# Halves of the convolution result split ahead of its transposes, low halves on GpSimd, weight pieces and x in a new order

## The reference

```python
h = conv1d(x, weight, taps=9, groups=4, pad=4) + (cond @ c_weight.T)[:, :, None] + bias
x = x + attention(h)      # q, k, v, o from 4-bit codes and scales, RoPE, 32 query heads, 8 kv heads
att = softmax(mlp(cond))  # 8 kernels mixed per sample
x = x + ffn(mix(att) @ x) # 512x512 base matmul plus top-2 of 28 LoRA experts
```

## Time and profile before

| | |
|---|---|
| median of 3 runs | 1658.37 us (1656.62 to 1659.03) |
| profiled execution, its own time | 1658.53 us |
| its span, first to last instruction | 1656.7 us |
| PE busy over the span | 1608.9 us, 97% |
| DVE, ACT, POOL busy | 84%, 76%, 68% |
| first block | 0 to 90 us |
| attention steps and the rest | 90 to 1656.7 us |

### The profile page before, as it was taken

How to read it: one execution, slowest core, us unless ns; L and a number is a source line. 1 busy time by engine, 2 the same in 40 slices (tenths; PEclk the granted TensorE clock), 3 DMA queues, 4 the chain that set the end, 5 groups by cost and what they waited for, 6 DMA issues and landing times.

```text
span 1656.7 us, 37682 instructions
## 1 busy us (share of the span) xinstructions
PE 1608.9 (97%) x14847; PEld 892.3 (54%) x14848; DVE 1397.7 (84%) x2174; ACT 1251.2 (76%) x2158; POOL 1130.7 (68%) x942
## 2 busy tenths in 40 slices
PE   8869999999999999999999999999999999899998
PEld 7825555555555555555555555555555555566665
DVE  4758888888888888888888888888888888888887
ACT  2348888888888888888888888888888888642221
POOL 1038777877787778777877787778777787623332
PEclk9989999999999999999999999999999999999999
DMA  8310010001000100000001000100000003012221
GB/s 302 93 45 27 14 33 2 27 14 33 1 27 15 33 1 27 14 33 2 27 14 33 2 27 15 33 1 24 17 1 27 25 2 89 27 64 89 78 79 50
DMA packets 31021, 60.83 MB, mean 37 GB/s; under 512 B 11368, under 2 KB 13992, under 8 KB 29568
## 3 DMA queue, kind: packets, MB, share of 16 engines
q1 hardware_dynamic: 30848, 58.42, 11.0%
HBM read 47.46 MB, written 10.95 MB: 35 GB/s over the span
## 4 chain that ended last, share of the span: by engine, by line
PE 66%; DVE 16%; POOL 6%; issue 5%; ACT 1%; DVEq 0%; POOLq 0%
PE banks L812 17%; PE banks L727 16%; PE banks L752 10%; DVE q_sin L1052 9%; PE banks L868 5%; PE banks L741 5%; DVE accT L1115 4%; PE banks L771 4%; PE banks L797 3%; PE banks L889 2%; DVE pT L1101 2%; PE banks L853 2%; POOL q_f L1312 2%; PE banks L839 1%; POOL k_f L1297 1%
## 5 line engine op out<-in xcount | busy, mean ns | idle before, releaser
L727 PE MATMUL banks<-hT,w_q 128*128 128x512 f16 x2048 | 549.3, 380 | 8.7 <-ACT banks L1432 3.7
L1432 ACT ACTIVATE banks<-banks,ratios 128x512 f32<-128x512 f32 x768 | 503.3, 663 | 65.9 <-PE banks L727 56.8
L812 PE MATMUL banks<-o_hl,w_o 128*128 128x512 f16 x2048 | 545.0, 380 | 3.0 <-ACT banks L1442 1.4
L1442 ACT ACTIVATE banks<-banks,ratios 128x512 f32<-128x512 f32 x768 | 480.8, 659 | 44.4 <-PE banks L812 41.6
L1312 POOL TENSOR_TENSOR q_f<-q_f,q_sin 128x1024 f32<-128x1024 f32 x128 | 301.4, 2355 | 100.8 <-DVE q_sin L1052 100.8
L812 PEld LDWEIGHTS banks<-o_hl,w_o 128*128 128x128 f16 x2048 | 180.7, 98 | 262.6 <-issue 35.3
L1052 DVE TENSOR_TENSOR q_sin<-banks,rope_q 64x1024 f32<-64x1024 f32 x256 | 312.7, 1222 | 8.2 <-POOL q_f L1312 2.5
L727 PEld LDWEIGHTS banks<-hT,w_q 128*128 128x128 f16 x2048 | 188.8, 98 | 240.4 <-ACT banks L1432 39.4
L1043 DVE TENSOR_SCALAR banks<-banks,ratios 128x512 f32<-128x512 f32 x192 | 145.2, 756 | 58.8 <-PE banks L741 58.7
L752 PE MATMUL banks<-w_v,hT 128*128 128x128 f16 x3072 | 194.1, 220 | 0.0
L752 PEld LDWEIGHTS banks<-w_v,hT 128*128 128x128 f16 x3072 | 178.2, 98 | 21.7 <-issue 0.2
(11 more groups left out here) (122 smaller groups left out, 1945.9 us busy)
## 6 DMA issues: line engine op xcount, KB each, us to landing
codes<-in_codes SPq DMA_DIRECT2D x40, 512.0 KB, 3.7
accT<-in_xT SPq DMA_DIRECT2D x8, 1024.0 KB, 12.9
hT<-in_x SPq DMA_DIRECT2D x32, 256.0 KB, 2.9
out<-codes SPq DMA_DIRECT2D x32, 256.0 KB, 2.0
v_s<-in_v_scales SPq DMA_DIRECT2D x8, 256.0 KB, 4.5
hT<-aggb_rows SPq DMA_DIRECT2D x1, 2048.0 KB, 7.0
f_src<-in_base_T SPq DMA_DIRECT2D x4, 256.0 KB, 10.1
base_rows<-f_hl SPq DMA_DIRECT2D x4, 256.0 KB, 3.1
```

The costliest lines, as they stand in the source:

```text
L727: mm = pe.matmul(banks[:, tile], w.q[:, n[2], kt * RF * HD + tile * HD:kt * RF * HD + (tile + 1) * HD], hT[:, n[1], kt, hp], start=kt == 0 ...
L812: mm = pe.matmul(o_bank(tile), w.o[:, p[2], h * D + tile * P:h * D + (tile + 1) * P], o_hl[:, op, h], start=h == 0 and op == 0, stop=op == ...
L1432: act.activation(banks[:, tile], banks[:, tile], ACT.Copy, scale=w.ratios[:, n[0], tile, kt:kt + 1]).then_inc(q_scaled[tile], 1)
L1442: act.activation(o_bank(tile), o_bank(tile), ACT.Copy, scale=w.ratios[:, p[0], RF + tile, h:h + 1]).then_inc(o_scaled[tile], 1)
```

## The change

**Split first.** After `add_ctx(n)`, ACT `high(n)` writes the fp16 high half of `h_f` into the new buffer `h_hl` (three units deep), and POOL writes the low half from it. PE's `turn(t)` then does eight fp16 transposes, four of each half, into one bank seen as fp16. Each finished bank is copied out whole, two copies by one engine: DVE for t % 8 in 0, 3, 6, ACT for the others. `turn(t)` is called for t = n − 4.

**Feeds.** x comes in 16 pieces of 512 KB, and the first two k of each group first. The feed-forward pieces go from n = 13 on, one every second n, and their buffers lie in the part of `xT` that is used up, so the first two loads wait for group 8 of the convolution. The code pieces 2 to 4 stand between them in SP's list, and POOL's dequantization stands between its low halves (n = 13 to 29).

**First step.** The first call of `body` is replaced on PE, ACT, DVE and POOL by a written-out list in which the four tiles and k take turns.

The diff, cut to its core:

```diff
+        def high(n):
+            u, half = n // 2, n % 2
+            act.wait_ge(h_added, n + 1)
+            if u >= 3:
+                act.wait_ge(hT_psum, 2 * u - 4)
+            cols = slice(half * HALF, (half + 1) * HALF)
+            act.activation(h_hl[:, u % 3, 0, :, cols], h_f[:, u % 2, :, cols], ACT.Copy).then_inc(h_hi, 1)
...
-        w.make_k(pool, 0)
-        w.make_v(pool, 0)
-        for j in range(1, PIECES):
-            w.make_qo(pool, 0, j)
-        pool.wait_ge(scale_step, 3)
-        w.make_rope(pool, 0)
+        for n in range(2 * UNITS):
+            u, half = n // 2, n % 2
+            cols = slice(half * HALF, (half + 1) * HALF)
+            pool.wait_ge(h_hi, n + 1)
+            pool.tensor_tensor(h_hl[:, u % 3, 1, :, cols], h_f[:, u % 2, :, cols], h_hl[:, u % 3, 0, :, cols],
+                               ALU.subtract).then_inc(h_low, 1)
+            if n == 13:
+                w.make_k(pool, 0)
+            if 14 <= n < 18:
+                w.make_v(pool, 0, (n - 14,))
+            if n in (19, 21, 25, 27):
+                w.make_qo(pool, 0, {19: 1, 21: 2, 25: 3, 27: 4}[n])
+            if n == 29:
+                pool.wait_ge(scale_step, 3)
+                w.make_rope(pool, 0)
...
-            pe.wait_ge(h_added, 2 * u + 2)
+            pe.wait_ge(h_low, 2 * u + 2)
             if t >= 3:
-                pe.wait_ge(hT_ready, t - 2)
-            for s in range(4):
-                mm = pe.transpose(bank[3 + t % 3][:, s * P:(s + 1) * P], h_f[:, u % 2, 4 * half + s], w.ident[:])
+                by = by_dve(t - 3)
+                pe.wait_ge(hT_by_dve if by else hT_by_act, taken(t - 3)[0 if by else 1])
+            for part in range(2):
+                for s in range(4):
+                    mm = pe.transpose(halves_bank(t)[:, part, s * P:(s + 1) * P], h_hl[:, u % 3, part, 4 * half + s], ident_h[:])
...
             if u >= 2:
-                dve.wait_ge(hT_psum, 2 * u - 2)
+                dve.wait_ge(h_low, n - 3)
...
-        def low(t):
-            dve.wait_ge(hT_hi, t + 1)
-            dve.tensor_tensor(in_hT(1, t), turned(t), in_hT(0, t), ALU.subtract).then_inc(hT_ready, 1)
+        def take(t):
+            if by_dve(t):
+                dve.wait_ge(hT_psum, t + 1)
+                for part in range(2):
+                    ins = dve.tensor_copy(in_hT(part, t), turned(part, t))
+                ins.then_inc(hT_by_dve, 1)
...
         for m in range(len(f_pieces)):
+            if 2 <= m < PIECES:
+                w.load_piece(sp, a, 0, m)
             store_f(m)
...
-            if 23 <= n < 23 + len(f_pieces):
-                f_lows(n - 23)
+            if 13 <= n < 13 + 2 * len(f_pieces) and n % 2:
+                f_lows((n - 13) // 2)
...
-        for n in range(STEPS):
+        for n in range(1, STEPS):
             body(steps[n + 2], steps[n + 1], steps[n])
```

More of the change, by code:

```diff
@@ L203, in prepare_and_convolve @@
     band_loaded = sem("band_loaded")
-    x_loaded = [[sem(f"x_loaded{k}{h}") for h in range(2)] for k in range(KT)]
+    x_loaded = [sems(f"x_loaded{k}", CGROUPS) for k in range(KT)]
     tables_loaded = sem("tables_loaded")
@@ L241, in in_hT, with halves_bank, turned, by_dve @@
         return hT[:, :, k, part].rearrange("p c (b s) -> p c b s", s=S)[:, :, :, s0:s0 + 4]
-    def turned(t):
-        return bank[3 + t % 3].rearrange("p (s c b) -> p c b s", s=4, c=CHUNKS)
+    def halves_bank(t):
+        return bank[3 + t % 3].bitcast(F16).rearrange("p (a n) -> p a n", a=2)
+    def turned(part, t):
+        return halves_bank(t)[:, part].rearrange("p (s c b) -> p c b s", s=4, c=CHUNKS)
+    def by_dve(t):
+        return t % 8 in (0, 3, 6)
+    def taken(t):
+        n = sum(by_dve(m) for m in range(t + 1))
+        return n, t + 1 - n
     f_pieces = [(a["base_T"][:, k], rows.base[:, :, k], slice(0, P), D) for k in range(KT)]
@@ L367, in _ @@
                 pe.matmul(bank[7][:, 0:S], att_T[:], kern[:, S * S:], start=True, stop=True).then_inc(agg_psum, 1)
-        turn(2 * UNITS - 2)
-        turn(2 * UNITS - 1)
+        for t in range(2 * UNITS - LAG, 2 * UNITS):
+            turn(t)
     @block.vector
@@ L441, in _ @@
         softmax()
+        dve.wait_ge(ident_loaded, 16)
+        dve.tensor_copy(ident_h[:], w.ident[:]).then_inc(ident_ready, 1)
         for n in range(2 * UNITS):
             add_ctx(n)
-            if n >= 3:
-                low(n - 3)
+            if n >= LAG:
+                take(n - LAG)
             if n == 3:
@@ L457, in _ @@
                 agg_lows(n - 10)
-            if 12 <= n < 18 + NKV // 2:
-                tables(n - 12)
-            if 23 <= n < 23 + len(f_pieces):
-                f_lows(n - 23)
-        for t in range(2 * UNITS - 3, 2 * UNITS):
-            low(t)
+            if n in (8, 9):
+                tables(n - 8)
+            if n >= 12 and n % 2 == 0 and n // 2 - 4 < 10:
+                tables(n // 2 - 4)
+            if 13 <= n < 13 + 2 * len(f_pieces) and n % 2:
+                f_lows((n - 13) // 2)
+        for t in range(2 * UNITS - LAG, 2 * UNITS):
+            take(t)
     @block.scalar
```

143 lines of the change are left out of this document (104 added, 39 removed).

## The result

| | before | now |
|---|---|---|
| median of ten runs | 1657.49 us (1655.67 to 1659.03) | 1652.36 us (1651.25 to 1654.13) |
| profiled execution, its own time | 1658.53 us | 1652.75 us |
| its span | 1656.7 us | 1650.9 us |
| mean granted clock of TensorE | 0.995 | 0.997 |

The ratio is 0.9971 (95% interval 0.9963 to 0.9979): 5.1 us faster, where 12.1 were forecast.

The account below looks back on a forecast made before the run. TensorE was taken to bound the first block's first part and starve in its second. Feed and start 5.6 + 2.0, moved turns 0.95, shorter end 2.15, first step 1.4: 12.1 off 1658.5, so 1646.4; 8-in-10 range 1642 to 1651.

Parts of the forecast that it names:

- start (conv 0): Front of the kernel: with a smaller first piece of x, group 0 starts at 7.4 instead of 9.39, 2.0 us.
- the feed: First block's later convolution groups: spreading the feed-forward pieces over every second group from 13 removes TensorE's starving, 5.6 us.
- the moved turns: Convolution loop: turns called two groups later leave two fewer ahead of the last convolution matmul, 0.95 us.
- conv 31 to the first projection: End of the first block: shortens from 7.7 us (82.6 to 90.32) to 5.6, a gain of 2.15 us.
- first step, to the first turn: First attention step: new order takes 10.2 us instead of 11.63 with the clock at its lower level, 1.4 us.
- Load of the engines: Densest eight groups, 16.2 us: VectorE 15.0, ScalarE 13.2; none reaches its limit, so TensorE stays the bound.
- VectorE and GpSimd hold each other up: Rival: VectorE's two-SBUF-input operations wait for GpSimd's subtractions in the first block, 3.4 us over, twice: 1653.2; chance 0.05.
- The tail: End of the first block: last convolution matmul at 74.0, projections at 79.6, with 1.5 us of TensorE standing.
- the slower case (dear transposes): Rival: fp16 transposes in the convolution loop cost as much as float32 ones, 15.0 us more: 1661.4; chance 0.04.
- stall for pieces 4 to 6: Rival in the feed: these pieces land late behind code pieces that wait for GpSimd, 7.5 us: 1653.9; chance 0.07.
- the start gains nothing: Rival at the front: the piece of x lands no earlier: 1648.4; chance 0.07.
- nothing is won: Rival: turns wait for GpSimd as they waited for VectorE, and the first block ends as now: 1658; chance 0.03.

Follow-up runs that it names:

- b3: b1 plus 32 GpSimd subtractions that nobody reads or waits for, its code jobs between them after groups 9 to 14; 1653.92 us, ratio 0.9974.
- b4: b1 plus unread GpSimd subtractions only for groups 0 to 8 and 17 to 31, code jobs in one go after group 9; 1648.43 us, ratio 0.9938.
- a1: Changed kernel with VectorE's low half of each feed-forward piece (`f_lows`) asked for one group later; 1647.56 us, ratio 0.9936 to the kernel before.
- a5: Changed kernel with `f_lows` one group later and `make_rope` after GpSimd's last low half; 1645.15 us, ratio 0.9931 to the kernel before.
- a3: Changed kernel with GpSimd's `make_rope` moved from behind low half 29 to behind the last one; 1650.75 us, ratio 0.9957 to the kernel before.
- a9: Changed kernel with x in eight pieces of 1024 KB again; 1655.13 us, ratio 0.9987 to the kernel before.
- b1: Kernel before with only the spread feed and VectorE's tables moved between: no split, old x, old first step; 1647.17 us, ratio 0.9939.
- a2: Changed kernel with the second input of `f_lows` read from a PSUM bank, leaving the right low halves out; 1649.26 us, ratio 0.9944 to the kernel before.
- a4: Changed kernel with `f_lows` one group later and its second input from PSUM, right low halves left out; 1645.83 us, ratio 0.9927 to the kernel before.
- b2: Kernel before with all of the change but the split: spread feed, x in sixteen pieces, new first step; 1641.75 us, ratio 0.9906.
- b5: b1 with the first attention step in the new order, x in eight pieces, no split; 1643.07 us, ratio 0.9909 to the kernel before.

## Why the prediction was wrong

The forecast's terms, and the same stretches in the profiles of before and now:

| gain, us | forecast | measured |
|---|---|---|
| start (conv 0) | 2.0 | 1.77 |
| conv 0 to conv 31 (the feed 5.6, the moved turns 0.95) | 6.55 | 1.89 |
| conv 31 to the first projection | 2.15 | −0.39 |
| first step, to the first turn | 1.4 | 1.96 |
| sum | 12.1 | 5.23 |

**Load of the engines: the step that failed.** The forecast summed busy time over eight groups, found 15.0 of 16.2 us for VectorE and 13.2 for ScalarE, and concluded "none reaches its limit, so TensorE stays the bound". That VectorE had time to spare was true (13.66 of 16.40 us busy where the stalls begin); that TensorE would therefore stay the bound was not. The sum adds up two lists that wait for each other as if each could use all its time. The loop between them took 4.7 us a turn and up to 5.8 where two groups give 4. That cost 25.35 − 21.99 = 3.4 us from conv 20 to conv 31 and left a backlog for the end.

The sum also priced eight pieces at the 0.68 of a trace in which GpSimd did nothing beside them; they took 1.15 to 1.26. This is the effect of the rival "VectorE and GpSimd hold each other up", with 0.05, and b3 and b4 show it. By the Trainium skill (SBUF — State Buffer, on who interferes with whom) a VectorE instruction with two SBUF inputs and one of GpSimd that reads SBUF exclude each other for a whole instruction; the lengths of 1.01 to 1.27 us agree with that. The forecast set it aside because "a mean wait of a third of that" would "all but vanish in the spare 1.2 us"; measured was near half of a subtraction, 0.5 us, and in the loop that counted. But the rival's own time, 1653.2, came from whole subtractions added to VectorE's load, 6.8 us. Nothing of that kind happened: a1 keeps the long operations and TensorE keeps its rate. That 1653.2 lies near the measured 1652.36 is luck.

**The tail, 5.6 forecast, 8.0 measured.** a5 shows 5.5, so the working was right for an empty list. `make_rope` at n = 29, which the forecast had in view in the diff and not in the chain, costs 0.8 with the backlog there (a3) and 1.5 without it (a1 against a5). The backlog makes up the rest.

**The moved turns, 0.95, came, and the longer group took most of them back.** Between the two profiles they can't be seen: conv 0 to conv 20 takes 44.47 us now and took 44.54 before, and this moves by 1 us from execution to execution. All sixteen profiled kernels show them. From conv 0 to conv 8 the ten with turns called two groups later take 18.8 to 20.0 us, mean 19.45, the six others 20.1 to 21.0, mean 20.35: 0.9 less. But a group takes 0.03 us more in the changed kernel, 0.7 over the groups behind conv 8. The forecast had put the group's length at no change.

**What was right.** The start within 0.2 (7.62 for 7.4), though the gain rests on one reading of before, as a9 showed. The eight fp16 transposes (0.45), by which the slower case (dear transposes) fell. (Its threshold was miscounted: 60 ns more than 56 is 2.1 times as much, not 1.9.) The feed itself: no stall for pieces 4 to 6. The first step: the lower clock at the hand-over, for 5 us of the projections (5.8 forecast), and 9.67 us to the first turn (10.2). That it was the lower level is in part luck: six of the sixteen profiled kernels kept the upper one there, b1 and b4 parted behind the same 5.28 us, and so the forecast's reason for its choice isn't shown. The rivals "the start gains nothing" and "nothing is won" fell by conv 0 at 7.62 and the measured 5.1 us.

**What was not asked.** The feed term, 5.6 us, was credited to the change as a whole. b1 has it without the split. With the old transposes and halves, the terms of the feed, the start and the first step stay, and the end, last convolution matmul to projections, takes 3.8 us (b1) instead of 5.6. The forecast priced the split at nothing because it lay beside TensorE; it never asked what the split was worth.

## What to carry to other kernels

When a change has several parts, price the one that adds work by itself and ask what the others would give without it; here the part with the most new code was the one that lost. Before work goes to an idle engine, look for loops: a wait from list A to list B and back, whose length per iteration is compared with the bound engine's, because summed busy time says nothing of it. A loop just over its budget needs only one link cut or shortened; here a second remedy gave nothing more in the stretch that the loop had bounded.

## What the runs showed of the hardware

**VectorE with two SBUF inputs beside GpSimd.** 0.68 us alone (683 ns in b1), 1.01 to 1.27 on the mean beside GpSimd's subtractions (b3, b4, the changed kernel), 0.688 with one input in PSUM (a2). Single ones vary more: the eight low halves of a1 took 0.66 to 1.65. Operations with an input in PSUM did not change: `add_ctx` took 690 before and 675 now. GpSimd pays too: its conversion of codes took 1.04 us in b1 and 1.37 in the changed kernel.

**The clock at the hand-over.** In the profiled executions TensorE's granted clock falls to its lower level, 1.2 GHz, at the hand-over or stays at 2.4 GHz. b1 and b4 stand for nearly the same time there, with 5.28 us from conv 31 to the projections in both. The stages of b1 and then of b4, one microsecond near the first projections:

```profile
83.00:84.00 1.00, 0.68 (x4) 0.33 (x5) 0.00 (x0) 0.88 (x3) 0.00 (x0) 1.00 0.82 315
```

```profile
83.00:84.00 1.00, 1.00 (x3) 0.44 (x4) 0.00 (x0) 0.00 (x0) 0.00 (x0) 0.50 0.58 217
```

b4 kept the lower level from 82 to 88 and took 11.70 us to the first turn, b1 9.69. Of the sixteen profiled kernels six kept 2.4 GHz at the hand-over (a3, a4, a5, b1, b2, b5). Four of these (a3, a4, a5, b5) fell to the lower level for 3 to 4 us, 11 to 12 us after the first projection, so part of what they had won came later all the same. Among b1's own executions the one with a mean clock of 1.000 took 1645.14 us and the three with 0.997 took 1646.30 to 1648.16. b5's don't follow that: 1643.34 and 1643.77 us at 1.000, 1642.77 and 1642.80 at 0.998 and 0.999. What decides the level was not found. In the first step it is worth 2.0 to 2.5 us (b4 and b1, the changed kernel and b5); what is left of that at the end of the kernel stays open.
